# Half of the expert gates by transfer from DRAM, and the tokens' low parts on GpSimd, in a hybrid of whitening, window attention and experts on one core

## The reference

```python
x = _L0_conv_ref(x, L0_conv_gamma, L0_conv_beta)          # whitening by Newton steps
t = _to_tokens(x)
t = t + _L1_attn_ref(_ln_t(t), L1_attn_gamma, L1_attn_beta)
t = t + _L1_ffn_ref(_ln_t(t), router_w, w1, b1, w2, b2)
...
logits = tokens @ router_w.T
probs = _softmax(logits)
rw, re = top_k(probs, 2);  rw = rw / rw.sum(-1)
combine = zeros((N, E)).at[arange(N)[:, None], re].set(rw)
out = tokens
for e in range(8):
    h = gelu(tokens @ w1[e] + b1[e])
    out = out + combine[:, e:e + 1] * (h @ w2[e] + b2[e])
```

## Time and profile before

| | us |
|---|---|
| median of 3 runs (1186.55 to 1189.57) | 1188.25 |
| the profiled execution's own time | 1198.36 |
| its span | 1196.5 |
| busy: PE / PEld / DVE | 1115.0 / 748.8 / 913.3 |
| busy: ACT / POOL | 614.6 / 146.7 |

### The profile page before, as it was taken

The page is one execution under the profiler, slowest core; times in us unless marked ns, Lnnn a source line. Parts: engine busy times, 40 slices in busy tenths (PEclk is TensorE's granted clock), DMA queues, the critical chain, the costliest instruction groups (busy, mean ns, idle before and its releaser), DMA issues.

```text
span 1196.5 us, 29077 instructions
## 1 busy us (share of the span) xinstructions
PE 1115.0 (93%) x9550; PEld 748.8 (63%) x9550; DVE 913.3 (76%) x2575; ACT 614.6 (51%) x975; POOL 146.7 (12%) x173
## 2 busy tenths in 40 slices
PE   7958999989899898989869999999999999999998
PEld 6836777777777777777655455555555555555553
DVE  6943678877777787878768877777787777777775
ACT  0015566656556565656435555555555555555553
POOL 6021222222222222222210000000000000000000
PEclk9957999999989898989759999999999999999999
DMA  9501121211211111211111222222222222222222
GB/s 291 195 22 27 48 60 50 61 48 46 61 44 51 47 54 47 54 47 35 37 54 39 69 69 68 68 68 69 69 69 69 69 68 68 68 69 69 69 69 47
DMA packets 136171, 78.69 MB, mean 66 GB/s; under 512 B 112416, under 2 KB 134176, under 8 KB 135344
## 3 DMA queue, kind: packets, MB, share of 16 engines
q1 hardware_dynamic: 127040, 64.78, 20.9%
q10 hardware_dynamic: 8064, 12.85, 2.9%
q0 software_dynamic: 1008, 0.43, 0.2%
HBM read 52.33 MB, written 25.69 MB: 65 GB/s over the span
## 4 chain that ended last, share of the span: by engine, by line
PE 64%; DVE 22%; ACT 5%; issue 5%; SPq 2%; DMA 1%; DVEq 0%; POOL 0%; ACTq 0%; POOLq 0%
PE p L1119 16%; PE p L1094 15%; PE p L1104 9%; DVE t_s L786 5%; PE p L1029 5%; PE p L1063 4%; PE p L934 3%; PE p L1041 3%; DVE sm L737 2%; PE p L927 2%; ACT prob L517 2%; DVE st L747 2%; PE p L1115 2%; DVE xn_s L780 2%; PE p L1058 2%
## 5 line engine op out<-in xcount | busy, mean ns | idle before, releaser
L546 ACT ACTIVATE arena<-p,b_s 128x896 f32<-128x896 f32 x224 | 225.4, 1007 | 245.9 <-PE p L1094 245.2
L843 DVE TENSOR_TENSOR arena<-arena,p 128x896 f32<-128x896 f32 x224 | 242.9, 1084 | 93.0 <-PE p L1104 89.8
L1119 PE MATMUL p<-arena,w_s 128*64 128x448 f32 x896 | 215.7, 560 | 0.3 <-DVE arena L843 0.3
L1094 PE MATMUL p<-thl,w_hi 128*128 128x448 f32 x448 | 165.0, 450 | 0.5 <-DVE thl L817 0.5
L1104 PE MATMUL p<-arena,selector 128*128 128x448 bf16 x448 | 124.7, 360 | 3.5 <-DVE arena L843 3.0
L1094 PE MATMUL p<-thl,w_lo 128*128 128x448 f32 x448 | 127.6, 366 | 0.0
L1104 PEld LDWEIGHTS p<-arena,selector 128*128 128x128 bf16 x448 | 25.5, 97 | 161.6 <-issue 116.1
L737 DVE TENSOR_REDUCE sm<-sq 128x14 f32<-128x896 f32 (+1 forms) x59 | 61.3, 1039 | 81.3 <-ACT sq L487 59.3
L1094 PEld LDWEIGHTS p<-thl,w_hi 128*128 128x128 f32 x448 | 85.8, 192 | 21.4 <-issue 1.0
L418 POOL TENSOR_TENSOR yb<-yb,bet 128x448 f32<-128x448 f32 x56 | 59.2, 1058 | 317.4 <-DVE xn_s L780 317.4
L1094 PEld LDWEIGHTS p<-thl,w_lo 128*128 128x128 f32 x448 | 84.9, 190 | 7.3
(11 more groups left out here) (174 smaller groups left out, 1817.5 us busy)
## 6 DMA issues: line engine op xcount, KB each, us to landing
tn_spill<-tnt_s ACTq DMA_DIRECT2D x56, 224.0 KB, 2.0
arena<-tn_spill SPq DMA_DIRECT2D x56, 224.0 KB, 3.4
t_s<-tn_spill SPq DMA_DIRECT2D x56, 224.0 KB, 2.5
arena<-in_x_dram SPq DMA_DIRECT2D x112, 96.0 KB, 2.1
out_dram<-arena SPq DMA_DIRECT2D x112, 96.0 KB, 1.8
resid<-in_x_dram SPq DMA_DIRECT2D x6, 1568.0 KB, 13.2
resid<-in_x_dram SPq DMA_DIRECT2D x6, 384.0 KB, 7.1
arena<-in_x_dram SPq DMA_DIRECT2D x112, 16.0 KB, 2.0
```

The source lines that it names most:

```text
L546: a.activation(hid[:, j % 2, :].rearrange("p (h n) -> p h n", h=H), (p34 if j % 2 == 0 else p56)[:, :, 0:CH], ACT.Gelu, bias=b1_s[:, j:j + ...
L843: v.tensor_tensor(gated[:, j % 2, :].rearrange("p (h n) -> p h n", h=H), hid[:, j % 2, :].rearrange("p (h n) -> p h n", h=H), p01[:, :, 0: ...
L1094: last = t.matmul(bank[:, h, 0:CH], w[:, 128 * j:128 * (j + 1)], thl[:, c, h, :], start=(k == 0), stop=(k == 1))
L1119: last = t.matmul(p2[64 * h:64 * h + 64, 0:CH], w2_s[:, j, :], gated[:, j % 2, h * CH:(h + 1) * CH], start=False, stop=(j == 3))
```

## The change

The gates of quarters 1 and 3 no longer come through TensorE. In the second stage's last steps and once in the third, the gates of each pair of images are transposed on TensorE (`turn_gates`, seven products from `comb`), copied by ScalarE to the new tile `turned`, and written to DRAM (`gate_spill`) by two transfers on ScalarE's queue (`spill_gates`). For each chunk SP then reads them back with `gates_in`, copied to all 64 partitions of each expert: six transfers for quarter 1 and six for quarter 3, into the tiles `gates[1]` and `gates[3]`. These have one buffer each, so `gates_in(g, j)` waits for `gate(g - 1, j)`. The VectorE `gate` of these quarters reads two SBUF tiles, and `spread` is left out for them. `low` moves from VectorE to GpSimd. SP's order is `gates_in(g - 1, 3)`, the token load, the row load, `gates_in(g, 1)`, the stores of chunk g - 2. `comb` is laid out by expert and block, so that its slices can be transposed. The loop on SP begins at chunk 8 instead of 2; chunks 2 to 7 are written out.

```diff
+    shares = nc.dram_tensor("gate_spill", (G, EM, NB * 128), f32).ap()
...
+        gates = {1: yb_tail[:, 0:H * CH], 3: tn_s[:, 0:H, :, :].rearrange("p s b c -> p (s b c)")}
+        turned = sb("turned", [128, 512])
...
+            def tokens_in(g, c):
+                wait(sp, s_hi, g - 1)
+                wait(sp, s_lo, g - 1)
+                sp.dma_start(tn_in[:, c, :].rearrange("p (h n) -> p h n", h=H),
+                             spill[g].rearrange("(h p) n -> p h n", h=H)).then_inc(s_ti[c], 16)
+
+            def gates_in(g, j):
+
+                wait(sp, s_gm, 4 * (g - 1) + j + 1)
+                for e in range(2):
+                    tile = gates[j][64 * e:64 * e + 64].rearrange("p (h n) -> p h n", h=H)
+                    row = shares[g, 2 * j + e]
+                    for h in range(H):
+                        sp.dma_start(tile[:, h, 0:TAIL].rearrange("p (b n) -> p b n", n=128),
+                                     row[0:2 * TAIL].rearrange("(b h n) -> h b n", h=H, n=128)[h].partition_broadcast(64)).then_inc(s_gi[j], 16)
+                    sp.dma_start(tile[:, :, TAIL:],
+                                 row[2 * TAIL:].rearrange("(h n) -> h n", h=H).partition_broadcast(64)).then_inc(s_gi[j], 16)
...
+            def step3(g, c):
+                gates_in(g - 1, 3)
+                tokens_in(g, c)
+                rows(g, c)
+                gates_in(g, 1)
+                store(g - 2, c)
...
+            for g in range(2, 8):
+                step3(g, g % 2)
+            sp.wait_ge(s_gd, 32 * NP)
+            with sp.Fori(4, G // 2) as i:
+                for c in range(2):
+                    step3(i * 2 + c, c)
...
+            def low(g, c):
+                wait(pool, s_lo, g)
+                wait(pool, s_hi, g + 1)
+                v.tensor_tensor(thl[64:128, c], tn_in[:, c].rearrange("p (h n) -> p h n", h=H),
+                                thl[0:64, c].bitcast(f32), ALU.subtract).then_inc(s_lo, 1)
...
+            def spill_gates(im):
+
+                act.wait_ge(s_gt, im + 1)
+                wait(act, s_gd, 32 * im)
+                for h in range(2):
+                    r, n = slice(64 * h, 64 * h + NB * EM), (CPI + 1 - h) // 2 * 128
+                    last = a.activation(turned[r, 0:n], p01[r, 1, 0:n], ACT.Copy)
+                last.then_inc(s_gts, 1)
+                act.wait_ge(s_gts, im + 1)
+                for h in range(2):
...
             for c in range(7):
                 step(G + c, c, lambda d, c=c: d > c)
+                spill_gates(c)
...
-            with act.Fori(2, G // 2 - 1) as i:
+            step3(4, 0, lambda d: True, 2)
+            spill_gates(NP - 1)
+            step3(5, 1, lambda d: True, 2)
+            with act.Fori(3, G // 2 - 1) as i:
...
                 wait(dve, s_g, u + 1)
-                wait(dve, s_c, u + 1)
                 wait(dve, s_l2, u - 1)
...
+                if j in gates:
+                    wait(dve, s_gi[j], 96 * (g + 1))
+                    v.tensor_tensor(gated[:, j % 2, :], hid[:, j % 2, :], gates[j], ALU.mult).then_inc(s_gm, 1)
...
                                 parts_step(g + 1, 1 - c, 4)
-                                low(g + 1, 1 - c)
...
+            def turn_gates(im):
+
+                pe.wait_ge(s_comb, im + 1)
+                wait(pe, s_gts, im)
+                for k in range(CPI):
...
-                    if has(0):
+                    if has(0) and j not in gates:
                         spread(g, c, j)
...
             for c in range(7):
                 step(G + c, c, lambda d, c=c: d > c)
+                pe.wait_ge(s_ys, G)
+                turn_gates(c)
```

More of the change, by code:

```diff
@@ L228, in hybrid_kernel @@
         s_ct, s_cts, s_ctd = sem("comb_t"), sem("comb_t_copied"), sem("comb_t_doubled")
+        s_gt, s_gts = sem("gate_weights_turned"), sem("gate_weights_copied")
+        s_gd = sem("gate_weights_spilled")
+        s_gi = {j: sem(f"gates_in{j}") for j in (1, 3)}
         s_h, s_g, s_c, s_gm = sem("hidden"), sem("gelu"), sem("weights_spread"), sem("gated")
@@ L334, in _, with store @@
+            def store(g, c):
+                wait(sp, s_fin, g + 1)
+                for tile, tokens in pieces(out_tokens, g, fin[:, c, :]):
+                    sp.dma_start(tokens, tile).then_inc(s_out[c], 16)
+            def step3(g, c):
[4 more added lines that the diff above has]
+                store(g - 2, c)
             for c in range(2):
                 sp.wait_ge(s_sp[c], 16)
-                step3(c, c, lambda d: d == 0)
+                tokens_in(c, c)
@@ L337, in _ @@
+            sp.wait_ge(s_gd, 32)
+            sp.wait_ge(s_t2, G)
+            sp.wait_ge(s_tn, G)
+            gates_in(0, 1)
+            sp.wait_ge(s_s, G)
+            for c in range(2):
+                rows(c, c)
+            sp.wait_ge(s_tnt, G)
+            gates_in(0, 3)
             for k in range(3):
@@ L339, in _ @@
                 sp.wait_ge(s_sp[k], 16 * spilled)
-            sp.wait_ge(s_s, G)
-            sp.wait_ge(s_t2, G)
-            for c in range(2):
-                rows(c, c)
-            with sp.Fori(1, G // 2) as i:
-                for c in range(2):
-                    step3(i * 2 + c, c, lambda d: True)
-            for c in range(2):
-                step3(G + c, c, lambda d: d > 0)
+            sp.wait_ge(s_gd, 32 * (NP - 1))
+            gates_in(1, 1)
+            for g in range(2, 8):
+                step3(g, g % 2)
+            sp.wait_ge(s_gd, 32 * NP)
+            with sp.Fori(4, G // 2) as i:
+                for c in range(2):
+                    step3(i * 2 + c, c)
+            gates_in(G - 1, 3)
+            for c in range(2):
+                store(G - 2 + c, c)
             for c in range(2):
@@ L436, in _ @@
             walk(pool, step, 7, G, 4, after)
+            def low(g, c):
[3 more added lines that the diff above has]
+                                thl[0:64, c].bitcast(f32), ALU.subtract).then_inc(s_lo, 1)
+            pool.wait_ge(s_zero, 3)
+            for c in range(2):
+                low(c, c)
+            with pool.Fori(1, G // 2) as i:
+                for c in range(2):
+                    low(i * 2 + c, c)
         @blk.scalar
@@ L901, in _ @@
                         parts_step(0, 0, k)
-                    low(0, 0)
             dve.wait_ge(s_comb, NP - 1)
@@ L1101, in spread @@
                     wait(pe, s_ctd, g + 1)
-                wait(pe, s_gm, u)
+                wait(pe, s_gm, u - 1)
                 for h in range(H):
@@ L1162, in _ @@
             step3(1, 1, lambda d: d <= 1)
-            with pe.Fori(1, G // 2 - 1) as i:
+            for g in range(2, 5):
+                step3(g, g % 2, lambda d: True)
+            pe.wait_ge(s_gm, 4 * 4 + 3)
+            turn_gates(NP - 1)
+            pe.wait_ge(s_gts, NP)
+            step3(5, 1, lambda d: True)
+            with pe.Fori(3, G // 2 - 1) as i:
                 step3(i * 2, 0, lambda d: True)
```

43 lines of the change are left out of this document (19 added, 24 removed).

## The result

The changed kernel takes 1415.2 us, the median of 4 runs (1413.48 to 1427.6); the kernel before beside it takes 1188.91 (1186.55 to 1195.13). The ratio is 1.192, with a 95% interval of 1.183 to 1.200. Slower was right, and 1415 lies in the range, but the forecast was +153 us and the kernel lost +226.

The account below looks back on a forecast made before the run. SP's issues and the ring were to set 12.7 us a chunk against 10.04: loop 128, written-out chunks 11, change of stage 11, eighth turn 3, in all +153 on 1188.25, so 1341 us; range 1263 to 1454.

Parts of the forecast that it names:

- step (c): SP's queue: 12 more gate issues a chunk at 0.70 us each, 12.4 us with the existing 4.0.
- Step (d): Loop from quarter 3's gate through gate issues, token load, `high`, gelu and back: 12.7 us a chunk.
- my formula (8.5 + six issues): Length of the ring from quarter 3's gate back to itself; under 10.04 us only for an issue every 0.25 us.
- the signs of the ring: New profile: ScalarE's `high` waits 1 us or more for the token load in every chunk.
- Step (a): TensorE: two of four spreads leave, 0.45 us each, 0.9 us a chunk, leaving 9.14 us of work.
- The rival with cheap issues: SP's issues turn out cheap, TensorE keeps the lead: 1153 us, chance 0.05.
- Step (b): `low` leaves VectorE, 1.08 us a chunk, for GpSimd, 2.1 us hidden; gives nothing, as VectorE isn't the bound.
- Step (e): DMA engines: the added 2048 packets and 0.92 MB a chunk fit, share 57% by packets, 50% by bytes.
- Step (f): End of the second stage: seven added turns of the gates cost 11 us, ends 4 and 20.
- the eighth turn: Chunk 5: TensorE and ScalarE wait for each other once, 3 us.
- The clock: Rival: TensorE at its lower clock sets the pace, 16.0 us a chunk, 1524 us; chance 0.12 shared with queue congestion.
- Contention of GpSimd and VectorE: Third stage: no cost in the forecast; with cheap issues up to 1 us a chunk, 1207 us; within a 0.03 chance.

Follow-up runs that it names:

- experiment 2: Kernel before with twelve more small transfers a chunk on SP's queue, into a tile nobody reads: 1383.67 us.
- experiment 5: Kernel after with only quarter 1's gates by six transfers, quarter 3's spread by TensorE again: 1229.87 us, ratio 1.037.
- experiment 10: Kernel after with one unbroken-row gate transfer per expert and quarter, unsorted, multiplication as two operations, token load first, row load last: 1172.36 us, ratio 0.9825 to before.
- experiment 9: Kernel after with gates by one transfer per expert and quarter from rows sorted in DRAM, row load last on SP: 1215.15 us, ratio 1.025.
- experiment 11: experiment 10 with the token load again behind the fourth quarter's gates in SP's queue: 1211.66 us, ratio 1.020.
- experiment 4: Kernel before with only `low` moved from VectorE to GpSimd: 1191.96 us, ratio 1.0015.
- experiment 12: experiment 10 with `low` back on VectorE: 1197.94 us, ratio 1.0035.
- experiment 1: Kernel after with the same gate transfers, each piece cut to 16 elements from chunk 2 on: 1422.12 us.
- experiment 7: Kernel after with a quarter's gates for both experts by one transfer, from rows sorted in DRAM: 1767.46 us, ratio 1.490.
- experiment 8: Kernel after with a quarter's gates by two transfers, one per expert to 64 partitions, from rows sorted in DRAM: 1219.52 us, ratio 1.028.

## Why the prediction was right in sign and short in size

**What bounds the kernel, and step (c).** Right: SP's issues became the limit. Undersized: this is the term that failed. I took 0.70 us for an issue from start to start; it is 0.81 (12 take 9.7 us; the call alone is 0.60). That is about midway between my 0.70, taken near the stores' 0.64, and the token load's 0.89, also to 64 partitions. The token load's call is itself shorter in the kernel after, 598 ns against 697. It is 0.60 behind the issues of gates and 0.70 behind stores (experiments 2 and 5); why is open. The other issues grew too: from the 4.0 us that I kept to 4.6, with the loop's branch in it (stores 2.84 and 3.32 in turn, token load 0.69, row load 0.84 against 0.45). 9.7 + 4.6 = 14.3 in place of 12 x 0.70 + 4.0 = 12.4. The range held because its upper end stood at the token load's price.

**Step (d), the ring.** Right as a mechanism, wrong as the limit here. By my formula (8.5 + six issues) it is 13.4 us with the measured issue, under the 14.3 of the sum; the slack of 1.3 us behind VectorE's gate puts it at 13.0. At the 0.70 that I took the ring (12.7) was the larger of the two limits; from 0.75 on it is the sum. With two issues in place of six the formula gives 8.5 + 2 x 0.65 = 9.8 (two start within 1.30 us in experiment 10); experiments 9 and 11 have 10.1 to 10.2, and moving the load out of the ring gives 9.49. I had named the signs of the ring, `high` waiting for over 1 us, as signs for (d); they don't tell it from the sum of issues, which delays the same load. Waits for a gate transfer, which I had named too, stand nowhere in the list of 700 to 1300 us.

**Step (a), two spreads.** 0.45 us each was too much. With TensorE full in both, a chunk takes 10.03 before and 9.49 in experiment 10; if all of that is the two spreads, one costs 0.27 us. It was hidden in the kernel after. The bound of 0.23, from start of the spread to start of the next first layer, was the better row. The rival with cheap issues would have gained 0.54 us a chunk and not 0.9.

**Step (b).** Worth nothing in the kernel before: right (experiment 4). As a general statement wrong: it is worth 0.6 us a chunk in experiment 12. That VectorE isn't the bound says nothing on where in its order an operation stands.

**Step (e), transport.** Right: 43% of the engines' time (50 to 57% forecast, at a shorter chunk), and the bytes don't matter (experiment 1).

**Step (f), and the written-out chunks.** The change of stage cost 6.7 us, 11 forecast. SP's loop begins with the stores of chunk 6, so I count from those of chunk 5, before and after:

```profile
695.14 2.39 SPq L332 DMA_DIRECT2D out_dram<-arena  x4
```

```profile
703.24 2.34 SPq L348 DMA_DIRECT2D out_dram<-arena  x4
```

Ahead of them the written-out chunks with the eighth turn cost 68.1 - 52.5 = 15.6, forecast 11 + 3. There it is not the sum: an issue follows the last at 0.65 us, and SP stands and waits, for VectorE's gates (the transfers of quarter 3 for chunks 2, 3 and 5 start within 0.03 us of the gate that they wait for) and for 3.6 us ahead of the row load at 686.30. So there it was waits of the kind of step (d) that set the time. The 48 chunks of the loop cost 206.5, and 128 were forecast. That is 78 too much, more than the 73 us that were missing in all, and it is (c).

**The rivals.** Cheap issues: ruled out by the call of 0.60 us. By the Trainium skill, page "DMA: Bandwidth & Descriptors", section "Issuing engines are not separate DMA queues", an engine's time for starting transfers is usually small beside the transfer. For one transfer the trace agrees (0.60 us, and 2.8 to its landing); experiment 2 shows what it comes to in a sum, up to 196 us. The clock: it did fall, to 0.86 on the mean, but TensorE was 78% busy, not over 95%, and had the pauses to take it in. Contention of GpSimd and VectorE: real, though rare, and not in the sum (below).

## What to carry over

Count the issues of each queue in a period and multiply them by the distance from start to start of the nearest shape, and the loop's branch with it; a queue whose sum is over the period is the limit, though no engine's busy share shows it. If the idea is good and the sum is bad, look for the same bytes in fewer calls, and check in the DMA view that the new shape still keeps the engines at work (experiments 7 and 8). In a queue, a load that another engine waits for goes ahead of everything that itself waits. Giving part of the issues to another engine's queue was not tried.

## What the hardware showed that I had not expected

**The shape of a transfer shows in its call, the bytes don't.** 64 partitions in three pieces: 604 ns with 384 elements for a partition, 604 with 48 (experiment 1). With one unbroken row of 896 elements the call is shorter, 468 to 533 ns at the median (experiments 8 to 12).

**One shape went through two engines only.** 2 x 64 rows of 3584 bytes in one transfer moved two packets at a time, at 52 GB/s; the same rows in two transfers of 64 moved at 153 GB/s on the mean, all traffic together (experiments 7 and 8). The number of engines at work is inferred from the share of 12.8%; the trace doesn't name the engine of a packet. That the outermost dimension, 2 or 64, decides it is my reading; the two runs also differ in the number of calls and the partitions of each. The issues behind the slow transfer took longer on the same queue: 12.91 us for four stores.

**GpSimd and VectorE shut each other out.** In the kernel before GpSimd does nothing in the third stage. In the kernel after a VectorE operation with two SBUF inputs met `low` four times, all before 700 us. At the start of the stage VectorE was held up:

```profile
618.53 2.08 POOL L475 TENSOR_TENSOR thl<-arena,thl 64x896 fp32r<-64x896 f32 x1 [15.24 <-ACT thl L620]
618.58 2.12 DVE L895 TENSOR_TENSOR arena<-arena 128x63 f32<-128x63 f32 x1
```

This operation takes 0.22 us elsewhere; it ended 0.1 us after GpSimd's did. In experiment 10 a multiplication of gates met `low` in the same way, at 663.75, and took 2.84 in place of 0.95, of which 0.82 lie behind the end of `low`. Where VectorE was first, it was GpSimd that took longer, 2.67 in place of 2.08, and VectorE's gate kept its 1.08:

```profile
686.19 1.08 DVE L905 TENSOR_TENSOR arena<-arena,yb_tail 128x896 f32<-128x896 f32 x1
...
686.57 2.67 POOL L475 TENSOR_TENSOR thl<-arena,thl 64x896 fp32r<-64x896 f32 x1 [10.03 <-ACT thl L620]
```

VectorE's multiplication of PSUM by SBUF kept its 1.09 us in all 51 meetings with GpSimd in experiment 10. That agrees with the rule of the Trainium skill, page "SBUF — State Buffer", section "Who interferes with whom", that two SBUF inputs on VectorE and GpSimd's reads exclude each other for a whole instruction. In the loop of experiment 10 they didn't meet, so 1207 us, the price that I gave this rival, was not paid.
